# Four blocks on eight images: new instruction orders for all engines and banks, and a bias added by GpSimd as a sum of two tiles

## The reference

```python
# L0: attention with pooled keys. theta, phi, g are projections of x; phi and g are max-pooled 2x2
attn = softmax(theta @ phi.T)                       # 256 x 64 for an image
x = x + sigma * ((attn @ g) @ w_o + b_o)
# L1: group norm (32 groups), one head of 128 channels
n = groupnorm(x) * gamma + beta
x = x + (softmax(q(n) @ k(n).T / sqrt(128)) @ v(n)) @ wo + bo     # 256 x 256
# L2: group norm (16 groups), eight heads of 16 channels
x = x + concat_heads(softmax(q @ k.T / 4) @ v) @ w_out + b_out    # 8 x (256 x 256)
# L3: Hartley transform over channels and width, flip, two-layer MLP in blocks of 16, soft threshold, transform back
...
x = y + x
```

## Time and profile before

| | us |
|---|---|
| median of 3 runs (lowest to highest) | 160.66 (159.46 to 163.44) |
| the profiled execution: its time | 159.53 |
| its span, first to last instruction | 157.7 |
| busy: TensorE matmul / weight loads | 149.7 / 114.7 |
| busy: VectorE / ScalarE / GpSimd | 104.8 / 108.7 / 50.1 |
| granted TensorE clock, all slices | full speed |

### The profile page before, as it was taken

How to read it: one execution, slowest core, us unless ns; L and a number is a source line. 1 busy time by engine, 2 the same in 40 slices (tenths; PEclk the granted TensorE clock), 3 DMA queues, 4 the chain that set the end, 5 groups by cost and what they waited for, 6 DMA issues and landing times.

```text
span 157.7 us, 3715 instructions
## 1 busy us (share of the span) xinstructions
PE 149.7 (95%) x1405; PEld 114.7 (73%) x1405; DVE 104.8 (66%) x265; ACT 108.7 (69%) x261; POOL 50.1 (32%) x115
## 2 busy tenths in 40 slices
PE   7989999999999999999989997999989999999992
PEld 4569889887777678766667765766677756799992
DVE  0577899999996898568956377639975611235543
ACT  3567979973688458983778942697358879567970
POOL 6467657534517442214020038010200050026100
PEclk9999999999999999999999999999999999999999
DMA  5960000000000000000000000000000020000003
GB/s 147 321 267 0 0 8 0 2 4 0 2 2 4 0 0 4 4 0 4 4 2 6 4 0 0 8 0 4 2 2 8 0 75 0 0 4 33 0 33 133
DMA packets 2800, 4.30 MB, mean 27 GB/s; under 512 B 352, under 2 KB 2272, under 8 KB 2784
## 3 DMA queue, kind: packets, MB, share of 16 engines
q1 hardware_dynamic: 2496, 3.87, 7.2%
q10 hardware_dynamic: 288, 0.21, 0.4%
HBM read 2.90 MB, written 1.05 MB: 25 GB/s over the span
## 4 chain that ended last, share of the span: by engine, by line
PE 71%; DVE 16%; ACT 5%; POOL 4%; issue 2%; DVEq 0%; ACTq 0%
PE psum L658 9%; PE psum L647 8%; PE psum L626 7%; DVE nmax L1148 6%; PE psum L573 4%; PE psum L553 3%; PE psum L685 3%; PE psum L699 3%; ACT pT L907 3%; PE psum L728 3%; PE psum L669 2%; PE psum L721 2%; PE psum L720 2%; PE psum L518 2%; PE psum L737 2%
## 5 line engine op out<-in xcount | busy, mean ns | idle before, releaser
L1148 DVE TENSOR_REDUCE nmax<-psum 128x4 f32<-128x1024 f32 x32 | 38.3, 1217 | 6.7 <-PE psum L626 6.7
L907 ACT ACTIVATE pT<-psum 128x1024 f32<-128x1024 f32 x32 | 31.6, 1027 | 4.7 <-PE psum L647 4.4
L626 PE MATMUL psum<-qk 16*128 16x256 f32 (+1 forms) x256 | 18.1, 397 | 0.0
L647 PE MATMUL psum<-qk 32*128 32x256 f32 (+1 forms) x256 | 18.0, 398 | 0.1
L332 POOL COPY zE<-zE 128x17 f32<-128x17 f32 x8 | 1.6, 198 | 46.1 <-ACT zE L924 46.1
L658 PE MATMUL psum<-pT,vaug_all 128*32 128x256 f32 x256 | 16.0, 383 | 0.0
L626 PEld LDWEIGHTS psum<-qk 16*128 16x128 f32 (+1 forms) x256 | 11.7, 184 | 4.4 <-DVE nmax L1148 1.5
L647 PEld LDWEIGHTS psum<-qk 32*128 32x128 f32 (+1 forms) x256 | 11.6, 184 | 3.9 <-issue 1.6
L326 POOL TENSOR_TENSOR rstd<-vare,half 128x1 f32<-128x1 f32 x16 | 9.5, 591 | 14.7 <-DVE vare L1101 14.7
L382 POOL TENSOR_SCALAR mv<-mv 128x1 f32<-128x1 f32 x16 | 6.0, 375 | 24.7 <-DVE mv L1088 24.6
L658 PEld LDWEIGHTS psum<-pT,vaug_all 128*32 128x32 f32 x256 | 7.3, 109 | 6.4 <-issue 2.2
(11 more groups left out here) (160 smaller groups left out, 352.5 us busy)
## 6 DMA issues: line engine op xcount, KB each, us to landing
out<-x SPq DMA_DIRECT2D x8, 128.0 KB, 1.9
tab<-in_weights SPq DMA_DIRECT2D x1, 708.0 KB, 7.8
tab<-in_weights SPq DMA_DIRECT2D x1, 576.0 KB, 5.4
x0T<-in_xT SPq DMA_DIRECT2D x4, 128.0 KB, 3.1
x0T<-in_xT_rest SPq DMA_DIRECT2D x1, 512.0 KB, 6.2
tab<-in_weights SPq DMA_DIRECT2D x1, 320.0 KB, 6.6
qk<-stage_all SPq DMA_DIRECT2D x16, 8.0 KB
tab<-in_weights ACTq DMA_DIRECT2D x1, 128.0 KB, 2.9
```

What stands on the lines that cost most here:

```text
L626: last = mm(bank[(b0, b1)[j // 2] + j % 2][:, u * TOK:(u + 1) * TOK], at[:, u, 0, :], at[:, :, 1, :], start=True, stop=True)
L647: last = mm(bank[(b0, b1)[j // 2] + j % 2][:, m * TOK:(m + 1) * TOK], at[:, m, 1, :], at[:, :, 0, :], start=True, stop=True)
L907: go(pT[g](i)[:, 2 * k:2 * k + 2].rearrange("p j m t -> p j (m t)"), pair(home["st", g, i][k]), ACT.Exp).then_inc(s["exp" + "EO"[g]], 1)
L1148: v.tensor_reduce(nmax2(i)[:, g, 2 * k:2 * k + 2, :], pair(home["sm", g, i][k]).rearrange("p j (u m) -> p j u m", u=TILES), AX.X, ALU.max, ...
```

## The change

All five lists are written in a new order, and the TensorE steps get new banks with the waits that belong to them. The set of steps is the same. One instruction is another: `x2b_out` adds the bias column by `tensor_tensor` with the column broadcast over the 256 tokens, instead of by `tensor_scalar`. In SyncE's list the first store now stands ahead of the last two spreads. The diff, cut to its core:

```diff
@@ -281,9 +281,9 @@
             load_rest()
             load_table(sp.dma_start, 3)
             load_table(sp.dma_start, 4)
-            spread(0, 1); spread(0, 0); spread(1, 0); spread(1, 1); spread(2, 0); spread(2, 1); spread(3, 1)
-            spread(3, 0); spread(4, 0); spread(4, 1); spread(5, 0); spread(5, 1); spread(6, 1); spread(6, 0)
-            spread(7, 0); spread(7, 1); store(0); store(1); store(2); store(3); store(4); store(5); store(6); store(7)
+            spread(0, 1); spread(0, 0); spread(1, 1); spread(1, 0); spread(2, 0); spread(2, 1); spread(3, 0)
+            spread(3, 1); spread(4, 1); spread(4, 0); spread(5, 0); spread(5, 1); spread(6, 0); spread(6, 1); store(0)
+            spread(7, 1); spread(7, 0); store(1); store(2); store(3); store(4); store(5); store(6); store(7)
             sp.wait_ge(s["stored"], 16 * IMAGES)
 
         @block.gpsimd
@@ -315,7 +315,7 @@
                 if i == 0:
                     pool.wait_ge(s["o2_rd"], 1)
                 pool.wait_ge(s["x2"], i + 1)
-                gp.tensor_scalar(x2b(i), x0T(i), b_out2[:, :], None, ALU.add).then_inc(s["x2b"], 1)
+                gp.tensor_tensor(x2b(i), x0T(i), b_out2[:, :].to_broadcast((P, TOK)), ALU.add).then_inc(s["x2b"], 1)
 
             def inverse_deviation(i, layer, *marks):
                 after(marks)
@@ -392,22 +392,22 @@
                 last.then_inc(s["nb1"], 1)
 
             fill()
-            pg_out(0); phi_out(0); pg_out(1); phi_out(1); pg_out(2); scaled1(0); pg_out(3, ("gw_ps", 1)); phi_out(2)
-            bias_wide(); scaled1(1); scaled1(2); mean_square(0, 1); phi_out(3); inverse_deviation(0, 1); scaled2(0)
-            pg_out(4); pg_out(5); mlp_sums(); mean_square(1, 1); score_shift(0); inverse_deviation(1, 1); phi_out(4)
-            mean_square(2, 1); inverse_deviation(2, 1); phi_out(5); scaled2(1); pg_out(6); score_shift(1)
-            pg_out(7, ("gw_ps", 5)); phi_out(6); phi_out(7); scaled2(2); mean_square(0, 2); score_shift(2)
-            inverse_deviation(0, 2); mean_square(3, 1); inverse_deviation(3, 1); mean_square(4, 1); mean_square(1, 2)
-            inverse_deviation(4, 1); inverse_deviation(1, 2); score_shift(3); mean_square(2, 2)
-            inverse_deviation(2, 2); score_shift(4); mean_square(5, 1); mean_square(3, 2); inverse_deviation(5, 1)
-            x2b_out(0); inverse_deviation(3, 2); x2b_out(1); mean_square(6, 1); x2b_out(2); score_shift(5)
-            inverse_deviation(6, 1); x2b_out(3); mean_square(4, 2); score_shift(6); inverse_deviation(4, 2)
-            mean_square(7, 1); inverse_deviation(7, 1); wrap(0); z_sum(0); z_difference(0); score_shift(7)
-            mean_square(5, 2); inverse_deviation(5, 2); wrap(1); z_difference(1); mean_square(6, 2); x2b_out(4)
-            x2b_out(5); z_sum(1); inverse_deviation(6, 2); x2b_out(6); mean_square(7, 2); inverse_deviation(7, 2)
-            wrap(2); z_difference(2); z_sum(2); wrap(3); z_sum(3); x2b_out(7); z_difference(3); wrap(4)
-            z_difference(4); z_sum(4); wrap(5); z_sum(5); z_difference(5); wrap(6); z_sum(6); z_difference(6); wrap(7)
-            z_sum(7); z_difference(7)
+            pg_out(0); phi_out(0); pg_out(1); phi_out(1); pg_out(2); phi_out(2); scaled1(0); pg_out(3); phi_out(3)
+            bias_wide(); scaled1(1); scaled1(2); pg_out(4); phi_out(4); mean_square(0, 1); inverse_deviation(0, 1)
+            pg_out(5); scaled2(0); mean_square(1, 1); mlp_sums(); mean_square(2, 1); inverse_deviation(1, 1)
+            score_shift(0); inverse_deviation(2, 1); phi_out(5); scaled2(1); pg_out(6); scaled2(2); phi_out(6)
+            score_shift(1); mean_square(0, 2); inverse_deviation(0, 2); score_shift(2); mean_square(3, 1)
+            inverse_deviation(3, 1); pg_out(7); mean_square(4, 1); mean_square(1, 2); phi_out(7)
+            inverse_deviation(4, 1); score_shift(3); inverse_deviation(1, 2); mean_square(5, 1); mean_square(2, 2)
+            score_shift(4); inverse_deviation(2, 2); inverse_deviation(5, 1); x2b_out(0); x2b_out(1)
+            mean_square(3, 2); inverse_deviation(3, 2); score_shift(5); mean_square(6, 1); inverse_deviation(6, 1)
+            mean_square(4, 2); mean_square(7, 1); inverse_deviation(4, 2); x2b_out(2); inverse_deviation(7, 1)
+            score_shift(6); wrap(0); z_sum(0); z_difference(0); score_shift(7); x2b_out(3); mean_square(5, 2)
+            inverse_deviation(5, 2); wrap(1); z_difference(1); z_sum(1); x2b_out(4); mean_square(6, 2); x2b_out(5)
+            inverse_deviation(6, 2); mean_square(7, 2); inverse_deviation(7, 2); wrap(2); z_difference(2); z_sum(2)
+            x2b_out(6); x2b_out(7); wrap(3); z_sum(3); z_difference(3); wrap(4); z_sum(4); z_difference(4); wrap(5)
+            z_difference(5); z_sum(5); wrap(6); z_difference(6); wrap(7); z_sum(6); z_difference(7, ("a", 6))
+            z_sum(7)
 
@@ -739,55 +739,54 @@
-            keep_clock(11, 7); proj0(0, 0); proj0(1, 1); proj0(2, 2); s0(0, 0); proj0(3, 3); s0(1, 1); gwm(0, 4)
-            gwm(1, 5); gwm(2, 0, ("p0", 1)); p0t(0, 2, ("theta", 3)); fold_biases(6); o0(0, 2); s0(2, 1, ("p0", 2))
-            proj0(4, 3, ("theta", 4)); proj0(5, 4); gm1(0); p0t(1, 6); fold_values(1, ("p0", 3))
-            fold_biases2(6, ("p0T", 2)); proj0(6, 7); o0(1, 5); qk1(0, 1); v1m(0, 3, ("theta", 5))
-            s0(3, 4, ("theta", 6)); s1(0, 1); p0t(2, 0, ("gw", 3)); gwm(3, 3, ("v1", 1)); gm1(1); o0(2, 0)
-            fold_mlp(4, 2); proj0(7, 3, ("gw", 4)); qk1(1, 5); gm1(2); v1m(1, 1, ("p1", 1)); p1t(0, 7); s1(1, 5)
-            s0(4, 1, ("v1", 2)); qk1(2, 0); o1(0, 7); gwm(4, 3, ("theta", 8)); v1m(2, 1, ("p0", 5))
-            gwm(5, 0, ("q1", 3)); p0t(3, 6); s1(2, 2, ("fold1_rd", 1), ("c_rd", 1)); gwm(6, 6, ("p0T", 4)); o0(3, 5)
-            p1t(1, 3, ("gw", 5)); gm2(0); fold_out2(4); s0(5, 0, ("gw", 6)); s0(6, 6, ("gw", 7)); s0(7, 1); o1(1, 3)
-            gm1(3); p0t(4, 2, ("p1", 3)); qk2(0, 7); o0(4, 2); p1t(2, 6); sm(0, 0, 4, 0, ("xn1", 4))
-            qk1(3, 6, ("p1T", 3)); gwm(7, 7, ("qkO", 1)); gm1(4); gm2(1); v1m(3, 6, ("q1", 4)); s1(3, 7, ("gw", 8))
-            o1(2, 6, ("v1", 4)); sm(0, 1, 0, 4, ("nmaxE", 2)); qk1(4, 2); qk2(1, 3); v1m(4, 7, ("p1", 4)); gm2(2)
...
-            sm(3, 1, 6, 4, ("nmaxE", 7)); pv(1, 1, 2, ("stage", 3)); am(0, 0, ("nmaxE", 8)); o1(5, 1)
-            st(2, 1, 2, 6, ("oTO", 2), ("nmaxO", 7)); ot(1, 0, ("aneg", 1)); ym(0, 4, ("nmaxO", 8)); x2t(1, 5)
-            nt(3, 0, ("on", 2)); gm2(5); ont(1); v3(0, 4); st(2, 0, 6, 2, ("expO", 6))
-            sm(4, 1, 0, 4, ("xn2", 6), ("stage", 4)); qk2(5, 6, ("expE", 5)); v2m(4, 7)
-            st(3, 0, 0, 2, ("nmaxO", 9), ("expE", 6)); o2(1, 7, ("vaug", 5)); p1t(6, 6, ("qkO", 6))
-            st(3, 1, 0, 4, ("expE", 7), ("nmaxO", 10)); zm(1, 7); o1(6, 6); sm(4, 0, 0, 2, ("expO", 7))
-            pv(2, 1, 4, ("expO", 8)); pv(2, 0, 7, ("z", 2)); sm(5, 0, 4, 0, ("oTO", 3), ("nmaxE", 9)); ot(2, 7)
...
-            ym(4, 6, ("z", 8)); v3(3, 5); am(7, 7); ym(5, 4, ("aneg", 7)); om(3, 6, ("yneg", 5))
-            v3(4, 7, ("aneg", 8)); ym(6, 5); ym(7, 6, ("xout", 4)); om(4, 4, ("yneg", 6)); v3(5, 5, ("yneg", 7))
-            v3(6, 7); v3(7, 6); om(5, 4, ("xout", 5)); om(6, 7); om(7, 6)
+            keep_clock(11, 7); proj0(0, 0); proj0(1, 1); proj0(2, 2); gwm(0, 0, ("theta", 1)); s0(0, 3); proj0(3, 4)
+            s0(1, 1); gwm(1, 2, ("theta", 3)); gwm(2, 5); s0(2, 3, ("p0", 1)); fold_biases(6); p0t(0, 7)
+            gwm(3, 1, ("p0", 2)); proj0(4, 0); o0(0, 3); p0t(1, 7); proj0(5, 4, ("theta", 4))
+            fold_values(2, ("gw", 2)); gm1(0); p0t(2, 5, ("gw", 3)); o0(1, 7); s0(3, 6); o0(2, 5)
+            fold_biases2(2, ("vo_rd", 1)); qk1(0, 3); s0(4, 4, ("theta", 6)); v1m(0, 0); gm1(1); s1(0, 3)
+            proj0(6, 1, ("gw", 4)); gm1(2); proj0(7, 0, ("v1", 1)); fold_mlp(4, 2); qk1(1, 7); v1m(1, 5, ("xn1", 3))
+            qk1(2, 3, ("p1", 1)); p1t(0, 7, ("q1", 2)); s1(1, 6); o1(0, 7); s1(2, 3); p0t(3, 1, ("theta", 7))
+            gwm(4, 2); s0(5, 0, ("theta", 8)); gm2(0); v1m(2, 5); gwm(5, 1, ("p0T", 4)); o0(3, 6); s0(6, 2, ("gw", 5))
+            qk2(0, 7); fold_out2(0, ("p0", 6)); gm1(3); p1t(1, 3, ("p1", 3)); sm(0, 0, 0, 4, ("o2_rd", 1))
+            p0t(4, 3, ("p1T", 2)); qk1(3, 6); p1t(2, 7, ("qkO", 1)); o1(1, 3, ("p0T", 5)); o0(4, 2)
+            sm(0, 1, 4, 6, ("nmaxE", 2), ("p1T", 3)); o1(2, 0); gm1(4); v1m(3, 1); s1(3, 4, ("nmaxO", 1))
+            p0t(5, 1, ("v1", 4)); gwm(6, 5); gm2(1); nt(0, 6); v2m(0, 1, ("p0T", 6)); s0(7, 7); v1m(4, 2)
+            o0(5, 1, ("vaug", 1)); qk1(4, 5, ("gw", 7)); qk2(1, 3); s1(4, 6); gm1(5); gm2(2); p1t(3, 7, ("p0", 8))
...
+            gm2(4); o2(0, 1, ("q1", 7)); s1(6, 2); v1m(6, 1, ("x3", 1)); gm1(7); st(1, 0, 6, 4, ("expO", 4))
+            zm(0, 3, ("xn2", 5)); sm(2, 0, 6, 0, ("expE", 3), ("xn1", 8)); pv(1, 1, 3, ("z", 1)); am(0, 2, ("p1", 7))
+            qk2(4, 3, ("oTO", 2)); sm(3, 0, 6, 4, ("nmaxE", 5)); qk1(7, 2, ("aneg", 1)); pv(1, 0, 0)
```

(53 more changed lines are left out.)

116 lines of the change are left out of this document (54 added, 62 removed).

## The result

The changed kernel takes 161.74 us (median of 7 runs, 161.65 to 161.97); the kernel before, beside it on the same chip, 159.53 (7 runs). The ratio is 1.0127, with a 95% interval of 1.0098 to 1.0157: 2 us slower, where I had forecast no change with a small gain. The changed time lies in my range of 156.6 to 162.4, but above the bounds of my own forecast (158.0 to 161.2), in the part that I had taken in for rival 2.

The account below looks back on a forecast made before the run. TensorE's list was taken as the bound, with 15.6 us of waits open to reordering. Head -0.5, VectorE +0.6, gm2(5) +0.75, v3(0) -0.3 and am(1) -1.0 sum to -0.45: 159.4 us, 80% range 156.6 to 162.4.

Parts of the forecast that it names:

- rival 2: VectorE's 2.45 us of earlier work are not covered and TensorE stops at v2m(2): 162.0 to 163.1 us, chance 0.12.
- VectorE front-loads: VectorE does eight steps earlier, delaying v2m(2) by 0.6 us; the qk2(0) wait, up to 0.7 longer, was not added.
- the VectorE term: TensorE waits at v2m(2) for VectorE's eight earlier steps: +0.6 us, bounds 0 and +2.45.
- Head, -0.5: Up to qk1(0), still starting at 15.1 us, TensorE has more work already done: -0.5 us, bounds 0 and -1.0.
- VectorE's eight steps, +0.6: Eight steps ahead of nmax2_out(1, 1, 1), 2.45 us, partly covered by TensorE work before v2m(2): +0.6 us.
- `gm2(5)`, +0.75: Near 80 us, gm2(5) has less TensorE work ahead, 1.95 instead of 2.71, so waits longer: +0.75 us, lower bound 0.
- `v3(0)`, -0.3: Near 80 us, v3(0) moves 12 us of TensorE work later and its wait of 0.31 goes: -0.3 us.
- `am(1)`, -1.0: z_sum(1) moves ahead of two x2b on GpSimd, so TensorE's 1.02 us idle before am(1) goes: -1.0 us.
- `x2b` at 0.72 us, off the path: GpSimd's new two-tile sum takes 0.72 us instead of 952 ns, bounds 0.40 and 0.95; by itself it gains nothing.
- the +2.45 at `v2m(2)`: Rival 2's main term: TensorE stops at v2m(2) for all of VectorE's earlier work, +2.45 us.
- the +0.7 at `qk2(0)`: Less TensorE work between gm2(0) and qk2(0) lengthens that wait by up to 0.7 us; only rival 2 counts it.

Follow-up runs that it names:

- e8: Old lists with the new two-tile sum, qk2(0) moved ahead of o1(1), gm1(3) and p0t(4) in TensorE's list; 160.86 us, ratio 1.0086.
- e14: Old lists with the new two-tile sum, one VectorE maximum, nmax1_out(3), made twice; 159.11 us, ratio 0.996.
- e5: Changed kernel's lists for steps starting before 24 us, then the old lists, new two-tile sum throughout; 159.85 us, ratio 0.9989.
- e1: Old lists for steps starting before 33 us, then the changed kernel's lists with its two-tile sum; 160.94 us, ratio 1.009.
- e13: Kernel before with only x2b changed to the sum of two tiles, old lists kept, second run of this edit; 158.79 us, ratio 0.9932.
- e10: Changed kernel with x2b back in its old one-tile-and-column form, new lists kept; 161.79 us, ratio 1.0128.
- e7: Changed kernel with p1_scaled reading one SBUF tensor and a column, part of the computation left out; 160.69 us, ratio 1.0043.
- e9: Old lists with the new two-tile sum, p1_scaled reading one SBUF tensor and a column, part of the computation left out; 158.42 us, ratio 0.9924.
- e12: Changed kernel with p1t(1) on a free bank ahead of qk2(0), and p1c(1) ahead of qkE(0) on ScalarE; 163.09 us, ratio 1.018.

## Why the prediction was wrong

**The step that failed** is the second one under "VectorE front-loads": "this wait grows by up to 0.7. I do not add it: while TensorE stands here VectorE works ahead, so the later wait for the same engine shrinks." Its size is wrong, and the recovery could at best have held for the +0.6 of the VectorE term.

*Its size.* I compared the TensorE work between `gm2(0)` and `qk2(0)`, 2.0 against 1.33, with a chain of 2.2 us. I did not look one step back, where the work between `o1(0)` and `gm2(0)` shrinks too, from 2.97 (`s1(2)`, `o0(3)`, `p1t(1)`, `v1m(2)` and small ones) to 1.42 (`s1(2)`, `p0t(3)`, `gwm(4)`, `s0(5)`): `gm2(0)` itself now waits 0.28, with the interval ahead of it 0.54 over the least. And the chain is not 2.2 here. From `gm2(0)` at 26.32 to `qk2(0)` at 29.05 it is 2.73, since the power meets `p1_scaled(1)`. In the new VectorE list `p1_scaled(1)` stands right behind `variance_eps(0, 2)`; both lists were there to be read, and the cost of such a meeting was in the old trace too (a power of 0.94 at 41 us). In all, the stretch from 20 to 25 grew by 1.80 (1.10 of it at `qk2(0)`, the rest at the steps behind, `gm1(3)` with a wait of 0.26 among them) and the interval ahead of `gm2(0)` by 0.54 more, where I had a bound of 0.7 and put nothing into the sum.

*Its recovery.* For a third of the 0.93 us that TensorE stands, VectorE stands too: it waits for the same power (0.46 idle in the row of `xn` above). Only behind that does it go on with image 3, and `gm1(3)` still waits for it. e8 made the stall alone, in the old lists, and nothing of 1.95 us came back; e14 took 0.68 us from VectorE at 36 us, 0.60 came through at once and 0.36 came back only behind 45 us. I had written the reason down myself, VectorE busy 9.96 of 10, and used it only for the next term. What my sentence may have right is small: the later wait for VectorE, which I had at +0.6, did not show, and the stall may have taken its place. It could give back no more than that.

The other steps:

- *Head, -0.5.* Right as far as I walked it: -0.48 at 10 us of work (3.84 to 4.30 in the ledger's five profiles with the new head, 4.48 to 4.94 in the six with the old). `qk1(0)` starts at 15.53, not 15.1, with `o0(2)` ahead of it. I stopped there; up to 20 the new lists lose 0.84 more than the old, 0.54 of it at `gm2(0)`, the rest in waits of 0.2 to 0.3 (`qk1(0)`, `gm1(2)`, `v1m(1)`). By e5 the head as a whole costs 1.1 us instead of winning 0.5.
- *VectorE's eight steps, +0.6.* Not to be seen: +0.08 from 25 to 45, and `v2m(2)` at 49.66 does not wait. The largest wait of 40 to 50 us is `gm1(5)`, 0.26 at 43.98. Without the stall, in e1, 1.35 more than in e13 appeared from 25 to 45, part of it from the join. That fits two terms that are alternatives, of which I kept the smaller one; no run has the new order there without either stall or join.
- *`gm2(5)`, +0.75.* The wait is there, 0.62 at 82.83 instead of about 1.0; its interval grew by 0.36. Half the size, because VectorE was earlier than I allowed.
- *`v3(0)`, -0.3, and `am(1)`, -1.0.* Both waits are gone, 0.5 and 0.9 us of the ledger.
- *Not counted.* `sm(2, 0)` at 69.85 waits 0.48 for ScalarE (the interval ahead of it is 0.74 over the least), and 0.3 are lost ahead of `sm(1, 0)`. ScalarE between 50 and 110 us was the list that I had compared only by its sums, and the longest of these waits are for it. They eat what `am(1)` and `v3(0)` gave: +0.01 from 45 to the end, where my terms make -0.55.
- *`x2b` at 0.72 us, off the path.* It takes 0.61. Off the path in the new lists (e10, no difference), not in the old ones (0.9 us), as the row could have told: two of them stood in front of `z_sum(1)`.

The Trainium skill's two figures that I weighed there ("GPSIMD Engine Reference", sections 3.1 and 4.1: about 2.6 cycles an element for a sum with two tensor inputs, roughly line rate for one input) would make the new form the slower one. The runs contradict that order: 0.61 us for the new form in e13 and in the kernel after, 0.95 and 0.93 for the old one in the kernel before and in e10, all on 128x256.

Rival 2 had the nearest time, 162.0 to 163.1 against 161.7, and the right condition, that in the middle there is nothing to spare. That the time comes so near is luck: of its terms, the +2.45 at `v2m(2)` was not there, `gm2(5)` had half its size, and the +0.7 at `qk2(0)` was far too small. Its place was wrong: the stall is 20 us ahead of `v2m(2)` and has to do with a chain, not with the count of VectorE's steps. By the ledger, the 2.7 us between my -0.45 and the measured 2.25 are +1.80 from 20 to 25, +0.84 from 10 to 20, +0.56 behind 45 us, and -0.52 from 25 to 45.

## What to carry to other kernels

When an order is changed, walk every chain of one item through all its engines (here x2, mean square, variance, power, xn, `qk2`), with the work that lies beside each of its links in the new lists, and start one link earlier than where the chain seems short. Where the second engine is busy nearly all of the window (here 9.5 of 10 and more), do not count on a stall of the first being made up: put it into the sum in full until a row shows slack. And split a change into instruction and order before believing either, both ways round: here the instruction won 0.9 us in the old orders and nothing in the new ones, and the orders lost 3.0 with it and 2.3 without.

## What the runs showed of the hardware

- A GpSimd step that starts while VectorE runs `p1_scaled`, a `tensor_tensor` with two tensors in SBUF, ends behind it, by a time that depends on the kind of step and not on when it started. The power on 128x1 takes 0.56 us alone; at 27.35, beside `p1_scaled` until 28.00, 1.08, ending 0.43 behind it, and at 40.98 in the kernel before 0.94, ending 0.42 behind. A mean square takes 0.34 alone and 0.68 to 0.76 beside one, ending 0.21 behind, five times in these two kernels. Seven such meetings in the kernel after, two in the kernel before and in e13. With one tensor and a column on VectorE the same ends are measured, 0.21 for four mean squares (e7) and 0.42 for a power (e9); only the power that starts 0.04 behind is back at 0.57 (e7). The Trainium skill states this ("SBUF — State Buffer", section "SBUF: two separate sides"): VectorE with two SBUF inputs, or in a mode that uses two ports, and GpSimd take a shared pair of ports as an exclusive lock for a whole instruction, and whoever starts first has it. The trace agrees for GpSimd steps that start 0.04 to 0.19 us behind the two-tensor form.
- The other way round the trace agrees in part. `normalised` on VectorE takes 0.42 us alone and 0.69 where an `x2b` of 0.61 us started just ahead of it (e13, 48.10 and 50.52). But where `x2b` (0.95 us) had started 0.53 ahead of `p1_scaled` in the kernel before, at 47.92, `p1_scaled` took its usual 0.68, and a power that started 0.03 ahead of one, at 31.54 in the kernel after, lengthened neither.
- A fall of the granted clock for some microseconds costs 1 us and more here. With `p1t(1)` moved (e12) TensorE stood 0.34, 0.26 and 0.49 us between 28 and 31 us, and in the profiled run the clock then fell to 0.80 and 0.85; the four runs of six with such a mean clock (0.989) took 1.3 us more than the two without. That the gaps are the cause is not shown: the kernel after, with 0.93 and 0.26 there, kept its clock in all seven runs, and the kernel before had a mean clock below 0.99 in 9 of the 26 runs beside e12.
